# Image 6 placed as a rounded part and a rest, and the upper probabilities turned earlier, in a vision tower with eight experts

## What is computed

```python
h = _L0_tok_ref(x, L0_tok_scharr)
h = _layernorm(h + _L0_attn_ref(h, Wq, bq, Wk, bk, Wv, bv))
h = _layernorm(h + _L0_ffn_ref(h, Wr, W1, W2))
# in the expert layer
flat = idx * cap + jnp.minimum(pos, cap - 1)
disp = jnp.zeros((E * cap, D), t.dtype).at[flat].add(t * kept[:, None])
h = jax.nn.relu(jnp.einsum('ecd,edf->ecf', disp.reshape(E, cap, D), W1))
```

## Time and profile before

| | |
|---|---|
| median of 3 runs | 243.0 us (242.95 to 243.71) |
| profiled execution | 243.3 us |
| its span in the trace | 241.6 us |
| mean granted TensorE clock | 0.988 |
| TensorE busy | 228.2 us, 94% |
| VectorE, ScalarE, POOL busy | 76%, 63%, 38% |

### The profile page before, as it was taken

The page is one execution under the profiler, slowest core; times in us unless marked ns, Lnnn a source line. Parts: engine busy times, 40 slices in busy tenths (PEclk is TensorE's granted clock), DMA queues, the critical chain, the costliest instruction groups (busy, mean ns, idle before and its releaser), DMA issues.

```text
span 241.6 us, 4974 instructions
## 1 busy us (share of the span) xinstructions
PE 228.2 (94%) x1654; PEld 220.2 (91%) x1654; DVE 182.9 (76%) x550; ACT 151.7 (63%) x357; POOL 92.9 (38%) x172
## 2 busy tenths in 40 slices
PE   6999999999999999799999999999999999999940
PEld 5999999999999999659999999999999999999940
DVE  6788797878879799978576876868778688689650
ACT  5337567787778787757685676675766757665100
POOL 7001227484746656767100025230252302523472
PEclk9999999999999999999999999999999999999995
DMA  5935984164797111201899709055090650100100
GB/s 165 273 110 152 279 273 130 48 217 175 216 365 251 43 50 36 82 5 47 275 363 382 246 12 375 18 198 184 8 369 31 194 186 3 48 0 24 36 4 0
DMA packets 28234, 35.48 MB, mean 147 GB/s; under 512 B 2643, under 2 KB 25154, under 8 KB 28210
## 3 DMA queue, kind: packets, MB, share of 16 engines
q1 hardware_dynamic: 26050, 31.71, 40.5%
q0 software_dynamic: 1744, 3.47, 3.9%
q10 hardware_dynamic: 416, 0.00, 0.1%
HBM read 26.97 MB, written 9.47 MB: 151 GB/s over the span
## 4 chain that ended last, share of the span: by engine, by line
PE 87%; issue 3%; DVE 3%; POOL 3%; ACT 1%; POOLq 1%; DMA 0%; ACTq 0%; DVEq 0%
PE bank L1485 16%; PE bank L1487 15%; PE bank L1486 15%; PE bank L1556 14%; PE bank L1573 5%; PE bank L1610 5%; POOL out_dram L685 2%; PE bank L1626 2%; PE bank L1822 2%; PE bank L1765 2%; PE bank L1731 2%; PE bank L1584 2%; PE bank L1628 1%; PE bank L1627 1%; PE bank L1650 1%
## 5 line engine op out<-in xcount | busy, mean ns | idle before, releaser
L1397 DVE SCALAR_TENSOR_TENSOR h_lo<-bank,h_hi 128x320 fp32r<-128x320 f32 x58 | 28.4, 491 | 24.4 <-ACT h_hi L970 21.4
L970 ACT ACTIVATE h_hi<-bank 128x320 fp32r<-128x320 f32 x58 | 25.4, 438 | 33.8 <-PE bank L1487 33.8
L1485 PE MATMUL bank<-einT_hi,w_hi 128*128 128x320 f32 x128 | 40.5, 317 | 0.0
L1486 PE MATMUL bank<-einT_lo,w_hi 128*128 128x320 f32 x128 | 39.5, 309 | 0.0
L1487 PE MATMUL bank<-einT_hi,w_lo 128*128 128x320 f32 x128 | 39.5, 309 | 0.0
L1108 DVE TENSOR_TENSOR w_lo<-w_raw,w_hi 128x1024 fp32r<-128x1024 f32 x31 | 37.7, 1216 | 0.0
L1485 PE MATMUL bank<-h_hi,w_hi 128*128 128x320 f32 x112 | 35.1, 313 | 0.0
L1486 PE MATMUL bank<-h_lo,w_hi 128*128 128x320 f32 x112 | 34.6, 309 | 0.0
L1487 PE MATMUL bank<-h_hi,w_lo 128*128 128x320 f32 x112 | 34.6, 309 | 0.0
L685 POOL DMA_INDIRECT out_dram<-tokens_mem,images x21 | 22.7, 1082 | 29.1 <-ACT tokens_mem L988 21.8
L881 ACT ACTIVATE w_hi<-w_raw 128x1024 fp32r<-128x1024 f32 x32 | 33.7, 1053 | 0.0
(11 more groups left out here) (251 smaller groups left out, 572.9 us busy)
## 6 DMA issues: line engine op xcount, KB each, us to landing
w_raw<-in_L_ffn_W_dram SPq DMA_DIRECT2D x16, 1024.0 KB, 7.9
images<-in_x_dram SPq DMA_DIRECT2D x7, 768.0 KB, 5.2
dispatched<-blank SPq DMA_DIRECT2D x4, 645.0 KB, 9.8
out_dram<-lone SPq DMA_DIRECT2D x8, 256.0 KB, 7.0
images<-dispatched SPq DMA_DIRECT2D x6, 258.0 KB, 5.5
images<-dispatched SPq DMA_DIRECT2D x3, 387.0 KB, 8.7
images<-in_x_dram SPq DMA_DIRECT2D x2, 384.0 KB, 4.2
out_dram<-tokens_mem,images POOLq DMA_INDIRECT x21, 2.9
```

The source lines that it names most:

```text
L970: act.activation(hidden_halves(n)[0], hidden_bank(n)[:, 0:CAP], ACT.Relu).then_inc(h_hi_ready, 1)
L1397: dve.scalar_tensor_tensor(lo, hidden_bank(n)[:, 0:CAP], 0.0, hi.bitcast(F32), ALU.max, ALU.subtract).then_inc(h_ready, 1)
L1485: pe.matmul(to, ah, bh, start=first, stop=False)
L1486: pe.matmul(to, ah, bl, start=False, stop=False)
```

## The change

Image 6 is no longer placed by four float32 products. ScalarE copies its finished rows, rounded, into `t_hi` (a part of `h_hi`), POOL subtracts to get `t_lo`, and TensorE places both with float32r operands: eight products, all ahead of `count(L)`. The picks of image 6 are written as float32r into a part of `einT_hi`. Behind `count(L)` only image 7's four placing products are left, ordered by columns. The transpose of the upper probabilities moves from behind the second lower attention product to between the two. On POOL `scale_lone(6)` moves from behind the image loop to behind `scale_last_rows`, ahead of `scatter(6)`, and the subtraction stands ahead of `number_rows(7)`. Two products on constants stand ahead of the first late transpose and one behind the transposes; they write bank 2, which nothing reads then.

```diff
-            return sums[:, s, 0:CAP] if b == B - 1 else tokens_mem[:, s * CAP:(s + 1) * CAP]
+            return sums[:, s, 0:CAP] if b == B - 1 else einT_hi[:, 1, s, :]
...
+        t_hi, t_lo = h_hi[:, 0:SC, 0:D], h_lo[:, 0:SC, 0:D]
...
-                if i >= 1:
+                if 1 <= i < L:
                     scale_lone(i - 1)
+            pool.wait_ge(t_hi_ready, 1)
+            pool.tensor_tensor(t_lo, trow[:, (L - 1) % TR, :, 0:D], t_hi.bitcast(F32), ALU.subtract
+                               ).then_inc(t_lo_ready, 1)
             number_rows(L)
             scale_last_rows()
+            scale_lone(L - 1)
             scatter(L - 1)
             scatter(L)
             scale_lone(L)
...
             late_prob_t_top()
+            act.wait_ge(late_t_ready, SC)
+            act.activation(t_hi, trow[:, (L - 1) % TR, :, 0:D], ACT.Copy).then_inc(t_hi_ready, 1)
             route_exp(L - 1)
...
                 pe.matmul(bank[5][:, 0:XG], probT[:, 2 * P:3 * P], val[:, L % 2, 1, 0:XG], start=True, stop=False)
+                pe.wait_ge(late_probs_ready, 2)
+                pe.transpose(bank[3][:, 0:P], prob[:, 0, 0:P], ident[:, :]).then_inc(late_turned, 1)
                 pe.wait_ge(late_values_ready, SC)
...
+            def place_rounded():
+                b = L - 1
+                pe.wait_ge(pick_ready, SC)
+                for half, ready in ((t_hi, t_hi_ready), (t_lo, t_lo_ready)):
+                    pe.wait_ge(ready, 1)
+                    for c in range(DC):
+                        for s in range(SC):
+                            pe.matmul(bank[c][:, 0:CAP], half[:, s, c * P:(c + 1) * P], pick(b, s),
+                                      start=False, stop=False, skip_group_check=True)
...
+            def fill_wait(n):
+                for _ in range(n):
+                    pe.matmul(bank[2][:, :], xT_hi[:, 0, 0, 0:P], xT_hi[:, 0].rearrange("p c s -> p (c s)"),
+                              start=True, stop=True)
+
+            pe.wait_ge(xb_ready, B)
+            fill_wait(2)
             late_prob_t()
+            fill_wait(1)
             late_attend()
-            late_prob_t_top()
             late_attend_top()
             early_turn(0)
             early_turn(1)
-            place(L - 1, 0, 0)
-            place(L - 1, 0, 1)
+            place_rounded()
             count(L)
-            place(L - 1, 1, 0)
-            place(L, 0, 1)
-            place(L, 0, 0)
-            place(L - 1, 1, 1)
-            place(L, 1, 1)
-            place(L, 1, 0)
+            for c in range(DC):
+                for s in (1, 0):
+                    place(L, c, s)
```

More of the change, by code:

```diff
@@ L298, in vit_tower_kernel @@
         row_mean_ready = sem("row_mean_ready")
+        t_hi_ready = sem("t_hi_ready")
+        t_lo_ready = sem("t_lo_ready")
         w_lo_first_ready = sem("w_lo_first_ready")
@@ L1699, in late_attend @@
                           ).then_inc(late_attn_done, 1)
-            def late_prob_t_top():
-                pe.wait_ge(late_probs_ready, 2)
-                pe.transpose(bank[3][:, 0:P], prob[:, 0, 0:P], ident[:, :]).then_inc(late_turned, 1)
             def late_attend_top():
@@ L1718, in early_turn @@
                 ins.then_inc(early_turned, 1)
+            def place_rounded():
[7 more added lines that the diff above has]
+                                      start=False, stop=False, skip_group_check=True)
             def place(b, c, s):
[L1721 to L1724, removed]
+                if s == 1:
                     pe.wait_ge(pick_ready, SC + 1)
```

## The result

The changed kernel took 245.39 us as a median of 7 runs (244.72 to 245.87). The kernel before has a median of 243.64 in its 7 runs, and of 243.50 without one slow run of 379.68 us, which the ratio leaves out. The ratio is 1.0066, 95% interval 1.0037 to 1.0096: 1.6 us slower (0.9 to 2.3). The forecast was 0.9 us slower, with a median of 243.9 and a range of 242.6 to 244.9; 245.39 lies above it.

A forecast was written before the change was run, and what follows sets the result against it. TensorE, busy 94%, was taken to wait for expert 1's rows: scatters 1.64 us late against 0.9 us of slack give 0.84, taken as 0.9, whatever the head gained; 243.3 + 0.9 = 244.2 profiled, 243.9 as median, range 242.6 to 244.9.

The forecast's parts named there:

- What bounds the kernel: TensorE busy 94% of the span; the change lies in the thin end of the last image, ending with ten placing products in 3.10 us.
- Part 1: Upper probabilities turned between the two lower products: ScalarE's copy 0.28 us earlier, worth 0.16 us on the router's choice.
- Part 3: Placing image 6 by halves: 1.08 us leave the ten placing products; POOL gets a 1.32 us subtraction, ScalarE a 0.62 us copy.
- Part 2: Three products on constants in TensorE's holes: taken at nothing, bounds 0.24 us lost to 0.1 us gained.
- The head: Work up to the first expert: last upper rows 0.14 us later, placing 0.28 less, so 0.14 us gained.
- Part 4: POOL's queue with scale_lone(6) ahead of the scatters: first scatter 1.64 us later, expert 1's transposes 0.84 us later, taken as 0.9.
- the four scatters keep their pace: Step on POOL's late scatters: durations unchanged, so SP issues expert 1's load at 116.01 in place of 114.37.
- The rule against the change: Two-buffer operations on POOL and VectorE don't run together; applied to VectorE's ranks, it makes the head worth 0 to 0.14 us.
- Rival B: Expert 1's rows in time, only the head counts: 0 to 0.45 us gained, 242.55 to 243.0; chance 0.20.
- C: A short wait for expert 1's rows, some delay absorbed: 0.2 to 0.6 us lost, 243.2 to 243.6; chance 0.18.
- D: POOL slower, or transpose not earlier: power operations 1.05 to 1.31, another 0.6 to 1.0 us, 244.5 to 245.0; chance 0.12.

## Why the prediction was wrong, point by point

- **What bounds the kernel**: the ten entries of the earlier trace rows are ten records, which is five products, not ten. No term of the sum rests on it.
- **Part 1** was right in kind. By the square, ScalarE's copy came 0.26 us earlier (0.28 forecast), the lower residual 0.30 later (0.23), the upper 0.10 earlier (0.16). What I gave too little weight is that POOL's scales follow the lower one (0.32 later with the transpose alone); in the changed kernel the subtraction hides that, as Part 3 said.
- **Part 2**: nothing, as forecast, as far as one execution shows.
- **Part 3**: subtraction 1.18 us (1.32); the last four products were done at 105.98, ahead of the count at 106.06. **The head**: the last upper rows came 0.14 later (0.14) and the first rectified chunk 0.15 earlier (0.14).
- **Part 4**, where it failed. First scatter 1.55 later (1.64): right. `scale_lone(6)` 1.53, gap 0.40 (0.54): right. Then "the four scatters keep their pace": **this step was wrong by 1.0 us**. The second scatter took 1.99 us in place of 0.98, so the load went out 2.55 us later, not 1.64; it landed after 3.5, and the hole was 1.78, not 0.9. The mechanism and its place were forecast; the scatters' own change was put at nothing, and it measured 1.0 us.
- **The rule against the change** was read off the right rows, and then used for one VectorE instruction alone. It was not asked what a VectorE operation of two buffers that runs first does to POOL, though the scatters stood among three of these. Putting the new start times beside VectorE's rows would have raised the question: 109.46 + 1.40 = 110.86 for the second scatter, against a subtraction that began at 110.88 before, 110.74 with the head's 0.14. A margin of 0.1 us either way can't decide a forecast, but it makes a rival with a price of 1 us and a chance of its own, and none had that price for this reason.
- The rest of the miss is the level of the runs: the kernel before stood at 243.5 beside the changed one and at 243.0 in the runs shown at first. Of 2.4 us between 243.0 and 245.39, 0.5 are that, 0.9 were forecast, and the 1.0 left is about what the collision measured.
- Rival B fell (the rows were not in time), C too. D, 244.5 to 245.0, came nearest and still fell short of 245.39, and for another reason: not longer power operations (0.70) but a longer scatter.

## What to carry to other kernels

Of a moved step, lay the new start times of everything queued behind it beside the other engines' timelines, and not only add up durations: a collision of 0.1 us in phase was worth 1 us here. A wait with 0.9 us of slack is a bound like any other; the cheapest repair was not to undo the change but to let the waiting consumer stand one chunk later. Short indirect DMAs on POOL are best placed where VectorE does no long operation on two buffers in SBUF.

## What the runs showed of the hardware

A scatter that starts inside a VectorE subtraction of two SBUF buffers takes its own time, 0.97 us, plus what is left of that subtraction, less 0.1. The 0.1 is fitted to these rows. For the starts and ends shown: after 0.97 + (112.16 - 0.1 - 111.03) = 2.00, measured 1.99; one more operation 0.97 + (110.22 - 0.1 - 109.66) = 1.43 and 0.97 + (112.24 - 0.1 - 111.37) = 1.74, measured 1.41 and 1.72; before, the fourth, 0.97 + (112.10 - 0.1 - 111.78) = 1.19, measured 1.16. All 23 such scatters in the 13 traces that have these subtractions lie 0.01 to 0.04 us below that sum (own time 1.09 for the first of the four). One that starts just ahead of the subtraction is not held. The Trainium skill, SBUF — State Buffer, "Who interferes with whom", states that an exclusive lock is taken by whichever starts first; by that rule, the held scatters agree. The other way round these traces don't: before, the subtractions at 109.26 and 110.88 begin 0.04 and 0.38 us inside a scatter and take 0.81 and 1.22 us, no longer than those with no scatter beside them (0.81 with four more operations, 1.22 at 117.11 before). The longest are three that began 0.33 to 0.34 us inside one and took 1.28 to 1.29.

What stays open: the time from the end of the last scatter to the load behind it. It was 1.42 to 1.43 us in the six executions in which no such VectorE operation began while that scatter ran (before, after, no constants, the turn later with and without the change, four more operations). It was 1.74 to 2.26 in the seven in which a subtraction began 0.33 to 0.40 us behind the scatter's start, and 2.06 with the one-buffer operation 0.12 behind it. It looks like a second hold, on what the scatter writes later. For it speaks the third scatter after, with a subtraction 0.38 us behind its start: the profile gives it a landing after 2.8 us. Against it speaks the third before, with a subtraction just as far behind: 2.3 us. No run settled it. Nor is it settled why the ratio with one more small operation is above what its profiled execution lost.
